# Attention value product in one piece behind the second score tile

## What is computed

```python
scores = jnp.einsum('bhqd,bhkd->bhqk', q, k) * scale
scores = jnp.where(causal[None, None], -jnp.inf, scores)
attn = jax.nn.softmax(scores, axis=-1)
out = jnp.einsum('bhqk,bhkd->bhqd', attn, v)
```

## Time and profile before

| | us |
|---|---|
| runs: median (lowest to highest) | 918.73 (916.28 to 921.4) |
| profiled execution, span | 931.8 |
| attention stage in it, first to last product | 106 to 659 |
| TensorE busy over the span | 758.3 |
| VectorE busy | 632.4 |
| ScalarE busy | 514.0 |
| GpSimd busy | 338.3 |

### The profile page before, as it was taken

The page is one execution under the profiler, slowest core; times in us unless marked ns, Lnnn a source line. Parts: engine busy times, 40 slices in busy tenths (PEclk is TensorE's granted clock), DMA queues, the critical chain, the costliest instruction groups (busy, mean ns, idle before and its releaser), DMA issues. The chain is left out here.

```text
span 931.8 us, 17439 instructions
## 1 busy us (share of the span) xinstructions
PE 758.3 (81%) x5615; PEld 359.8 (39%) x5615; DVE 632.4 (68%) x1916; ACT 514.0 (55%) x1048; POOL 338.3 (36%) x517
## 2 busy tenths in 40 slices
PE   5886699999999899899999989899267589898900
PEld 2331233333343243243233324233056468787700
DVE  6998788787878778668779758873044436565556
ACT  3562267677668576467576656678145224344423
POOL 3773212222222331732321642231441605565532
PEclk9996599999999899889899979999679889999955
DMA  6469254313531432514414433011511224332172
GB/s 163 138 165 212 72 115 63 54 33 50 92 60 28 86 63 52 111 46 66 82 32 88 86 72 62 28 36 32 167 49 58 63 70 129 94 86 67 55 203 79
DMA packets 112346, 77.07 MB, mean 83 GB/s; under 512 B 44202, under 2 KB 95819, under 8 KB 112075
## 3 DMA queue, kind: packets, MB, share of 16 engines
q1 hardware_dynamic: 99408, 63.02, 31.1%
q0 software_dynamic: 4352, 8.99, 2.9%
q10 hardware_dynamic: 8498, 3.97, 1.7%
HBM read 46.89 MB, written 26.56 MB: 79 GB/s over the span
## 5 line engine op out<-in xcount | busy, mean ns | idle before, releaser
L1137 ACT ACTIVATE expT<-ps 128x512 f32<-128x512 f32 (+1 forms) x640 | 334.0, 553 | 180.9 <-PE ps L1342 165.9
L290 DVE CUSTOM_DVE_ANT_0 x_in<-ps,mask 128x1024 bf16<-128x1024 f32 (+7 forms) x512 | 365.4, 755 | 93.7 <-PE ps L279 82.1
L1342 PE MATMUL ps<-q_space,k_space 96*128 96x512 bf16 (+3 forms) x768 | 227.1, 339 | 17.5 <-issue 10.0
L279 PE MATMUL ps<-k_space,q_space 96*128 96x512 bf16 (+3 forms) x768 | 203.1, 351 | 34.3 <-DVE mx L290 26.6
L1315 PE MATMUL ps<-expT,vr 128*9 128x256 f32 (+1 forms) x2560 | 183.4, 369 | 2.0 <-POOL expT L1098 2.0
L1098 POOL TENSOR_SCALAR_AFFINE_SELECT expT<-expT 128x512 f32<-128x512 f32 x128 | 81.7, 651 | 239.0 <-ACT expT L1137 239.0
L1342 PEld LDWEIGHTS ps<-q_space,k_space 96*128 96x128 bf16 x768 | 62.4, 99 | 172.6 <-ACT expT L1137 90.6
L279 PEld LDWEIGHTS ps<-k_space,q_space 96*128 96x128 bf16 x768 | 66.3, 101 | 101.1 <-DVE mx L290 61.8
L1524 POOL DMA_INDIRECT expert_rows<-row_ring,tile_to x72 | 69.1, 960 | 74.0 <-issue 40.1
L1315 PEld LDWEIGHTS ps<-expT,vr 128*9 128x9 f32 x2560 | 41.7, 89 | 101.0 <-issue 59.1
L705 POOL DMA_INDIRECT sorted_rows<-rows,places x64 | 62.9, 983 | 40.3 <-DVE places L890 22.5
(11 more groups left out here) (194 smaller groups left out, 951.7 us busy)
## 6 DMA issues: line engine op xcount, KB each, us to landing
q_space<-q_parts SPq DMA_DIRECT2D x48, 192.0 KB
row_ring<-sorted_rows SPq DMA_DIRECT2D x72, 65.0 KB
k_space<-k_parts SPq DMA_DIRECT2D x32, 128.0 KB
q_parts<-parts SPq DMA_DIRECT2D x24, 128.0 KB, 2.3
k_parts<-parts SPq DMA_DIRECT2D x24, 128.0 KB, 2.8
k_space<-k_parts SPq DMA_DIRECT2D x16, 192.0 KB
v_ones<-v_st SPq DMA_DIRECT2D x8, 288.0 KB, 3.4
vr<-v_ones SPq DMA_DIRECT2D x16, 144.0 KB
```

The source lines that it names most:

```text
L279: last = nc.tensor.matmul(psw[:, at + lo:at + hi], qr[:, g % RING, hh, qi * P:(qi + 1) * P], kr[:, g % RING, hh, lo:hi], start=True, stop= ...
L290: last = nc.vector.tensor_tensor_reduce(out=unread[:, odd, col:col + width], in0=psw[:, 2 * CT * odd + col:2 * CT * odd + col + width], in ...
L1137: act.activation(expT[:, (NS * g + s) % PTN, hh, 0:width], ps[:, B_S + hh % 2, 0:width], ACT.Exp, scale=SCALE).then_inc(exp_ok, 1)
L1342: last = nc.tensor.matmul(ps[:, B_S + hh % 2, col:col + m], kr[:, g % RING, hh, kt * P:(kt + 1) * P], qr[:, g % RING, hh, q0:q0 + m], star ...
```

## The change

A step's product is no longer cut in halves. All its pieces are issued behind the second score tile (hh == PV_AT, which is 1), none behind the fourth. The waits ahead of the product (exponentials, mask, oT of the group before) stay ahead of it, and pv_done is incremented by the last matmul of it.

```diff
@@ -112,6 +112,7 @@
 LAG = 2
+PV_AT = 1
...
-                def product(g, s, part):
+                def product(g, s):
...
-                    cut = (len(pieces) + 1) // 2
-                    for i, (kt, q0, n, col) in list(enumerate(pieces))[slice(0, cut) if part == 0 else slice(cut, None)]:
+                    for i, (kt, q0, n, col) in enumerate(pieces):
...
-                    if part == (len(pieces) > 1):
-                        last.then_inc(pv_done, 1)
+                    last.then_inc(pv_done, 1)
...
-                            if hh % 2:
-                                product_behind(g, s, hh // 2)
+                            if hh == PV_AT:
+                                product_behind(g, s)
                 for s in range(NS - LAG, NS):
-                    for part in range(2):
-                        product(G - 1, s, part)
+                    product(G - 1, s)
```

More of the change, by code:

```diff
@@ L1294, in item @@
                         last.then_inc(wide_ready, 1)
-                def product(g, s, part):
+                def product(g, s):
                     half, segs = STEPS[s]
                     first, end = s in (0, HALF0), s in (HALF0 - 1, NS - 1)
[L1301 to L1306, removed]
+                    pe.wait_ge(exp_ok, GH * NS * g + GH * (s + 1))
+                    if DIAGS[s]:
+                        pe.wait_ge(masked, NDIAG * g + DIAG_UNTIL[s])
+                    if first:
+                        wait(pe, oT_ok, 2 * (g - 1) + half + 1)
                     pieces = [(kt, q0 + o, min(CT // 2, n - o), col + o) for kt, q0, n, col in segs
                               for o in range(0, n, CT // 2)]
-                    cut = (len(pieces) + 1) // 2
-                    for i, (kt, q0, n, col) in list(enumerate(pieces))[slice(0, cut) if part == 0 else slice(cut, None)]:
+                    for i, (kt, q0, n, col) in enumerate(pieces):
                         at = q0 - CT * half
@@ L1318, in product, with product_behind @@
                                 stop=end and i == len(pieces) - 1)
-                    if part == (len(pieces) > 1):
-                        last.then_inc(pv_done, 1)
-                def product_behind(g, s, part):
+                    last.then_inc(pv_done, 1)
+                def product_behind(g, s):
                     if s >= LAG:
-                        product(g, s - LAG, part)
+                        product(g, s - LAG)
                     elif g > 0:
-                        product(g - 1, s - LAG + NS, part)
+                        product(g - 1, s - LAG + NS)
                 for p, e in enumerate(WIDE):
```

## The result

The changed kernel takes 935.06 us (median of 4 runs, 931.01 to 937.26), before 920.07 us in the runs beside it. The ratio is 1.020, with a 95% interval of 1.015 to 1.025: slower by 18.5 us on 920 by the ratio, by 15 (1.016) if the two medians are divided. The interval stands clear of no change. The forecast was 935.7 us.

The account below looks back on a forecast made before the run. TensorE with its excursions was taken to bound the quiet groups. Terms 4.1 + 4.7 + 1 + 0 + 5 + 2.3 = +17 us, added to the median 918.73, gave 935.7 us; range 919 to 948.

Parts of the forecast that it names:

- The bound: Quiet groups 1 to 3: TensorE with its excursions bounds them, busy 29.37 of 29.90 us.
- the excursion: TensorE going from scores to product and back: 0.21 us without work each, 18 a group; 127 removed, 27 us.
- The loop: Score, exponential, next score on that bank: from a step's third score, next step's first waits to 1.08 us, second to 1.57.
- 3.1 us of waits a group: TensorE in a quiet group: waits the change opens, against 1.7 us of excursions saved; net +1.4 us in 29.9.
- group 15: Last group, bare of maxima: six 512-column steps go from 2.50 to 2.86 us, +2.3 us.
- groups 1 to 3: Groups without feed-forward side work, repeating exactly: 3 x 1.37 = 4.1 us longer, near 31.3 us each.
- 4.7 + 0 + 5: Groups 4 to 14: quiet-length steps +4.7 us, steps with side work 0, ScalarE's row normalizing +5.
- rival 2: Quiet steps lose +12 us, but 59 steps with side work keep 0.21 each, -12: 919 us, no change; chance 0.13.
- the term for the quiet steps: Groups 4 to 14: 51 of 110 steps have the quiet length and lengthen by 4.7 us together.
- the 0 + 5 us for the steps with side work: 59 steps: 0 taken (ends -12 and +8), plus 5 for ScalarE normalizing rows in six groups (ends 0 and 12).
- Rival 1: Maxima and side work fill the bare loop, only excursions count: 918.7 - 27 = 892 us; chance 0.07.
- Rival 4: ScalarE's side work at full price on the bare loop, product burst starves VectorE: +30, 949 us; chance 0.1.

Follow-up runs that it names:

- quarters: Kernel before, with the product in pieces of 128 columns, one behind each of the four scores: 1.055 of before, 984.13 us beside 932.5.
- at0: Changed kernel with the whole product behind the first score instead of the second (PV_AT 0): 1.037 of before.
- at2: Changed kernel with the whole product behind the third score instead of the second (PV_AT 2): 1.016 of before.
- at3: Changed kernel with the whole product behind the fourth score instead of the second (PV_AT 3): 1.030 of before.
- split_single: Kernel before, with the one-piece 256-column products of steps 2 and 9 split into two of 128, behind second and fourth scores: 1.001 of before.
- short_before: Kernel before, with each exponential made over half of its columns only, so the output is not the reference's: 1.005 of before.
- short_after: Changed kernel, with each exponential made over half of its columns only, so the output is not the reference's: 1.021 of before.
- three_after: Changed kernel with three PSUM banks for the score tiles instead of two, both query halves' products sharing one bank: 0.991 of before.
- three_moved: three_after with each item that stood just ahead of the product put behind the third score: 1.017 of before.

## Why the prediction was right

**The bound and the excursion** were read rightly: 0.21 us, 18 and 10 a group, shown by the changed kernel's own rows and by quarters. TensorE's waits in a quiet group of before were a little more than the "under 1 us" of the prediction: 0.80 and 0.44.

**The loop** of 1.08 and 1.57 us holds to a hundredth, and the lifted loop proves it the cause. 3.1 us of waits a group were forecast, 0.25 of it VectorE's; 3.24 were found, 0.23 of it VectorE's. The quiet group came to 31.50, not 31.3.

**The groups.** From the first score of each group to that of the next (group 15: to the last product), changed less before: group 0 +2.3 (forecast +1); groups 1 to 3 +4.7 (+4.1); groups 4 to 14 without 8 and 12 +8.7; group 15 +2.6 (+2.3, though six times 0.36 is 2.2). For groups 4 to 14 the forecast was 4.7 + 0 + 5 = 9.7. The sum agrees, but the parts do not, and part of the agreement is luck. Groups 6, 10 and 14 became shorter by 1.1 to 1.5 us, which looks like rival 2, and groups 9 and 11 longer by 2.9 and 3.1. These are the groups in which the granted clock changed. Groups 6, 9 and 13, before and then changed:

```profile
299.10:337.00 37.90, 34.36 (x278) 11.81 (x274) 29.39 (x99) 25.22 (x53) 11.19 (x23) 0.91 0.33 69
412.40:446.40 34.00, 32.06 (x289) 13.10 (x286) 27.07 (x91) 25.23 (x53) 9.35 (x20) 1.00 0.29 46
558.80:592.70 33.90, 31.96 (x288) 13.03 (x284) 26.96 (x91) 25.13 (x53) 9.36 (x20) 1.00 0.27 46
```

```profile
309.40:345.90 36.50, 32.26 (x275) 12.72 (x276) 28.50 (x95) 25.21 (x53) 11.37 (x23) 0.95 0.35 71
422.80:459.70 36.90, 32.85 (x285) 14.51 (x286) 27.22 (x91) 25.44 (x53) 9.33 (x20) 0.95 0.24 42
567.30:603.10 35.80, 31.55 (x285) 13.99 (x285) 27.21 (x91) 25.22 (x53) 9.33 (x20) 1.00 0.26 43
```

Groups 9 and 13 do the same work and took the same time before; in the changed kernel group 9, at 0.95, takes 1.1 us more. The groups of side work whose clock is the same in both profiles (4, 5, 7 and 13) all became longer, by 1.3 to 1.8 us. Step by step the two traces can be taken apart further. Of the 110 steps of groups 4 to 14, from third score to third score, 92 lie at the full clock in both: 58 of quiet length, which grew by 9.3 us in all, and 34 others, which grew by 2.7. The 18 that the lower clock touches in either profile shrank by 9.9 us together, 9.3 of that in groups 8 and 12; before has 17 us more at the lower level in these steps. So the term for the quiet steps was too small (it counts 51 of them; by this measure they are 61), the 0 + 5 us for the steps with side work too large as far as they can be compared, and what the lower clock and the stalls of groups 8 and 12 give back stands in no term. ScalarE's normalizing and the rest of the side work were not taken apart.

**Groups 8 and 12** became shorter by 0.1 and 6.7 us, which nothing in the forecast has. Both profiled executions stall in group 8, at different places, and before in group 12 as well (3.7 us ahead of the score at 543.02). In before, TensorE stood still for microseconds with all it waited for long done, while the DMA engines were 0.70 busy and the granted clock was 0.71; in the changed kernel it waited 4.2 us for a load of rows. The rows of before from 385 to 398 us and of the changed kernel at 414:

```profile
396.92 0.61 PE L1342 MATMUL ps<-q_space,k_space 96*128 96x512 bf16 x1 [2.51 <-issue]
...
385.00:398.00 13.00, 7.85 (x41) 2.18 (x40) 4.58 (x15) 4.75 (x9) 7.69 (x8) 0.71 0.70 144
```

```profile
414.17 1.11 PE L896 MATMUL ps<-identf,at 128*128 128x128 f32 x4 [4.20 <-DMA x_rows<-in_x]
```

With these two groups the attention grew by 11.5 us in the profiles, without them by 18.3; and the part behind the attention, which is untouched, took 273.3 us in the profile of before and 265.0 in that of the changed kernel. From these two the spans' difference of 3.4 us is made up. That part varies with the chip: it took 274 to 277 us in the four profiles of quarters, at0, at2 and at3, from one chip, and 263 to 267 in the three of split_single, short_before and short_after, from another. How the 15 to 18 us of the runs divide, which have no profile each, is not shown. Whether the difference is added to the median, as the prediction did, or the median is scaled makes little odds here: scaling gives 935.5 us.

**The rivals.** Rival 1 (the saving stands) fell with two banks: 3.0 us of waits against 1.7 saved. It comes true in part once the loop is lifted. Rival 2 (the steps with side work keep their 0.21 us each) does not hold where the clock is the same: those 34 steps grew. Rival 4's starved VectorE showed in three_after and three_moved, not in the changed kernel.

## What to carry to other kernels

A piece of work that stands in the shadow of a loop (score, exponential, next score on the same bank) is free there and may not be so elsewhere. Before merging two pieces to save their fixed cost, look for a place in the trace where one of them is already missing, and read the wait there. When such a merge fails, the buffer count is the thing to change: one bank more turned 2.0% slower into 0.9% faster. With two producer loops on one engine, lifting one bares the other; here it paid to pace the items of the second by their consumer's time. And two profiles are compared group by group only where their granted clock is the same.

## What the runs showed of the hardware

In at0 the granted clock fell to its lower level in the last group, with nothing changed but the place of the product. In the 5 us before it fell TensorE was busy 3.86 us, at the full clock; after it, 4.74 of 5 in each row, with less done (29 and 33 matmul instructions against 36). The same group kept the full clock in the changed kernel (1.00 in its last row above). So the engine looks fuller than before while it does less. That the waits made the clock fall is not shown. In the profiles of before and changed the stretches at the lower level lie, behind group 0, in groups 6, 7, 8, 10 and 14 of both, in 12 of before and in 9 and 11 of changed. Groups 9 and 13 above show what one costs: 1.1 us for a granted clock of 0.95 over a group.

Groups 8 and 12 held stalls of some us in the profiles of most of the kernels, at steps that differ from one to the next. In the stretch of before shown above the DMA engines were 0.70 busy. What holds the engines when all that they wait for is done was not tried and is open.
